# Retiming three edges of a selective scan in a two-layer decoder kernel on one Trainium2 core: a mask step, a bank order and a gate's activations change place

## The reference

```python
# sublayer 1: linear attention, 16 heads of 32
q, k, v = heads(x @ q_w.T + q_b), heads(x @ k_w.T + k_b), heads(x @ v_w.T + v_b)
qp, kp = elu(q) + 1, elu(k) + 1
kv = einsum('bhsd,bhse->bhde', kp, v)
z  = einsum('bhsd,bhd->bhs', qp, kp.sum(axis=2))
x1 = layernorm(x + (einsum('bhsd,bhde->bhse', qp, kv) / (z + 1e-6)) @ o_w.T + o_b)
# sublayer 2: selective scan over the context, gated by silu(x1)
u = silu(causal_conv4(ctx @ in_proj.T) + conv_b)
dt_low, Bm, Cm = split(u @ x_proj.T)              # 16 + 16 + 16 columns
dt = softplus(dt_low @ dt_proj.T + dt_proj_b)
state = state * exp(dt * A) + (dt * u) * B_t      # 512 steps, 512 channels, 16 states
y  = (sum_n state_n * C_n + D * u) * silu(x1)
x2 = layernorm(x1 + y)
```

## Time and profile before

| what | value |
|---|---|
| time, median of 3 runs | 2728.22 us (2726.62 to 2728.88) |
| the profiled execution | 2728.88 us, span 2727.2 us |
| busy share of the span | PE 93%, DVE 71%, ACT 47%, POOL 27% |
| mean granted TensorE clock | 0.974 of full speed |
| the stage of the scans | about 62 to 745 us |
| chain that ended last | PE 53%, DVE 27%, ACT 8%, issue 8%, POOL 3% |

### The profile page before, as it was taken

How to read it: one execution, slowest core, us unless ns; L and a number is a source line. 1 busy time by engine, 2 the same in 40 slices (tenths; PEclk the granted TensorE clock), 3 DMA queues, 4 the chain that set the end, 5 groups by cost and what they waited for, 6 DMA issues and landing times.

```text
span 2727.2 us, 30212 instructions
## 1 busy us (share of the span) xinstructions
PE 2534.4 (93%) x9938; PEld 1675.5 (61%) x9938; DVE 1944.2 (71%) x3609; ACT 1276.6 (47%) x2404; POOL 729.6 (27%) x721
## 2 busy tenths in 40 slices
PE   6999999989779998899999999999999998999997
PEld 2343433434367754577777776777777773688886
DVE  4899999899975578677778787778788785231332
ACT  4464554645433311476746665566646663121111
POOL 1446455556411255221212121121121110000000
PEclk8999999999989999899999999999999999999999
DMA  4112111112320301232323322332332215100000
GB/s 153 54 48 85 51 67 62 56 39 77 116 101 32 124 16 43 108 112 101 139 82 120 109 100 68 100 101 82 102 115 93 78 47 190 51 31 1 31 16 16
DMA packets 81606, 212.51 MB, mean 78 GB/s; under 512 B 8998, under 2 KB 17446, under 8 KB 77356
## 3 DMA queue, kind: packets, MB, share of 16 engines
q1 hardware_dynamic: 73196, 180.88, 20.0%
q0 software_dynamic: 5472, 21.01, 2.0%
q10 hardware_dynamic: 2784, 8.72, 0.9%
HBM read 164.11 MB, written 46.47 MB: 77 GB/s over the span
## 4 chain that ended last, share of the span: by engine, by line
PE 53%; DVE 27%; ACT 8%; issue 8%; POOL 3%; DMA 1%; DVEq 0%; SPq 0%; POOLq 0%; ACTq 0%
PE bank L729 13%; PE bank L1094 10%; DVE h L1890 6%; DVE val L2174 3%; PE bank L1269 3%; PE bank L1270 3%; PE bank L1273 3%; ACT p L1662 3%; DVE val L2167 3%; PE bank L1180 2%; PE bank L944 2%; PE bank L945 2%; PE bank L1203 1%; PE bank L1298 1%; PE bank L1299 1%
## 5 line engine op out<-in xcount | busy, mean ns | idle before, releaser
L2479 POOL TENSOR_TENSOR h<-du,Bb 128x1024 f32<-128x1024 f32 x128 | 313.0, 2448 | 220.8 <-DVE h L1898 220.3
L1890 DVE TENSOR_TENSOR_SCAN h<-bank,h 128x512 f32<-128x512 f32 x256 | 299.7, 1206 | 28.2 <-ACT bank L1443 20.9
L1443 ACT ACTIVATE bank<-dt,A 128x512 f32<-128x512 f32 x256 | 175.1, 690 | 304.2 <-DVE h L1890 302.8
L1662 ACT ACTIVATE p<-bank,sm,rq 128x512 f32<-128x512 f32 x256 | 195.9, 775 | 173.1 <-DVE sm L2303 173.1
L2557 POOL TENSOR_TENSOR rq<-rq,mhalf 128x4 f32<-128x4 f32 x64 | 84.6, 1321 | 690.7 <-DVE rq L2249 690.7
L729 PE MATMUL bank<-pT,v 128*128 128x512 f32 x512 | 230.2, 592 | 0.8 <-ACT pT L1325 0.8
L1898 DVE TENSOR_TENSOR h<-h,Cb 128x1024 f32<-128x1024 f32 x128 | 197.4, 1542 | 6.5
L944 PE MATMUL bank<-h,ident 128*128 128x512 f32 x256 | 148.0, 661 | 53.5 <-DVE h L1898 53.0
L282 POOL TENSOR_SCALAR rstd<-mv 128x1 f32<-128x1 f32 x80 | 23.6, 295 | 647.7 <-DVE mv L276 647.4
L2433 DVE TENSOR_TENSOR h<-bank,sg 128x512 f32<-128x512 f32 (+1 forms) x44 | 30.4, 690 | 227.5 <-PE bank L1273 227.5
L2299 DVE TENSOR_REDUCE sm<-bank 128x1 f32<-128x512 f32 x256 | 164.1, 681 | 2.9 <-PE bank L1094 2.6
(11 more groups left out here) (273 smaller groups left out, 6104.2 us busy)
## 6 DMA issues: line engine op xcount, KB each, us to landing
wxq_s<-wq_dram SPq DMA_DIRECT2D x48, 512.0 KB, 4.0
Bb<-bc_dram SPq DMA_DIRECT2D x32, 512.0 KB, 3.6
Cb<-bc_dram SPq DMA_DIRECT2D x32, 512.0 KB, 3.7
x_dram<-xo POOLq DMA_DIRECT2D x16, 1024.0 KB, 4.8
woh<-in_Wo SPq DMA_DIRECT2D x64, 256.0 KB, 2.6
xc<-x_dram SPq DMA_DIRECT2D x12, 1024.0 KB, 5.5
wxv_s<-wkv_dram SPq DMA_DIRECT2D x12, 1024.0 KB, 5.0
wxk_s<-wkv_dram SPq DMA_DIRECT2D x12, 1024.0 KB, 7.8
```

What stands on the lines that cost most here:

```text
L1443: act.activation(bank[2 + n][:, :], dt[:, c % 2, et, :], ACT.Exp, scale=A[:, et, 2 * w + n:2 * w + n + 1]).then_inc(dA_ready, 1)
L1662: act.activation(p4[:, t, :], bank[4 + t][:, :], ACT.Exp, bias=sm4[:, 4 + t:5 + t], scale=rq[:, hh % 2, 1, t:t + 1], accum_out=sm4[:, 8 + ...
L1890: dve.tensor_tensor_scan(h[:, s, n, :], bank[2 + n][:, :], h[:, s, n, :], 0.0, ALU.mult, ALU.add).then_inc(scanned, 1)
L2479: pool.tensor_tensor(h[:, G % HR, :, :], du[:, et:et + 1, :].to_broadcast([P, 2, S]), Bb[:, w % 2, :, :], ALU.mult).then_inc(dBu_ready, 1)
```

## The change

It has four parts, all in the first stage.

1. DVE masks kv 0 (three pairs of small instructions) after unit 15 and its query step, where it did so between the scans and the C product of unit 15.
2. In the bank order "xdbl" comes behind "kv" 1. PE computes kv 1 in unit 15 and xdbl in unit 16, the reverse of before.
3. On ACT `copy_xdbl` moves from unit 17 to unit 18 and `turned` 2 from unit 19 to unit 18, both behind the exponential n = 1. The four `relu_abs` move one place earlier each: units 20 and 21, after n = 0 and after n = 1.
4. `gate_x1` of a chunk stands at the end of its unit 31, before the exponentials of the next chunk's unit 0, where it stood behind both of them. `value` 2 stands between these two exponentials, where it stood behind both.

```diff
             list0(("q", c, 3), ("kv", c, 0))
             if more:
-                list0(("x", c + 1, 0), ("xdbl", c + 1))
+                list0(("x", c + 1, 0))
             list0(("kv", c, 1))
             if more:
-                list0(("x", c + 1, 1))
+                list0(("xdbl", c + 1), ("x", c + 1, 1))
             list0(("z", c))
...
# PE
-                    if U == 15 and more:
+                    if U == 15:
+                        keys_values(c, 1, (3,))
+                    if U == 16 and more:
                         in_xdbl(c + 1)
-                    if U == 16:
-                        keys_values(c, 1, (3,))
-                        if more:
-                            turn_x(c + 1, 1)
+                        turn_x(c + 1, 1)
...
# ACT, after the exponential n == 0
+                            if U == 0:
+                                value(c, 2)
...
-                            if U in (21, 22) and more:
-                                relu_abs(c + 1, 2 * U - 41)
+                            if U in (20, 21) and more:
+                                relu_abs(c + 1, 2 * U - 40)
...
# ACT, after the exponential n == 1
-                            if U == 0:
-                                if c:
-                                    gate_x1(c - 1)
-                                value(c, 2)
...
-                            if U == 17 and more:
+                            if U == 18 and more:
                                 copy_xdbl(c + 1)
-                            if U == 19 and more:
                                 turned(c + 1, 2)
                             if U in (20, 21) and more:
-                                relu_abs(c + 1, 2 * U - 40)
+                                relu_abs(c + 1, 2 * U - 39)
...
                                 if more:
                                     value(c + 1, 0)
                                     value(c + 1, 1)
-                                else:
-                                    gate_x1(c)
+                                gate_x1(c)
...
# DVE: out of unit(), between the scans and the C product
-                if U == 15:
-                    for g in range(3):
-                        key_value(c, g)
...
# DVE: behind the query step
                     if U == 15:
                         query(c, 3)
+                    if U == 15:
+                        for g in range(3):
+                            key_value(c, g)
```

## The result

| what | before | after |
|---|---|---|
| time, median of 10 runs | 2731.11 us (2726.62 to 2744.24) | 2745.19 us (2736.26 to 2754.51) |
| ratio | | 1.006, 95% interval 1.0042 to 1.0079 |
| profiled execution | 2728.88 us, span 2727.2 | 2739.87 us, span 2738.2 |
| mean granted TensorE clock in it | 0.974 | 0.973 |

The change makes the kernel slower by 0.6%. The ratio counts more executions than the first row: the changed kernel ran 19 times, with a median of 2750.0 us, and the ten of the row by themselves would give 1.005. The forecast was 2734.7 us, in a range that ended at 2743: the sign is right and the size too small.

What follows compares the result with a forecast made beforehand. DVE and PE were both taken as nearly full, with PE's chain binding units 15 to 22. 2 x 1.95 + 0.35 - 0.9 + 3.05 = +6.4 us on 2728.22 gave 2734.7 us, range 2722 to 2743.

Steps and rivals of the forecast that it cites:

- Parts 1 and 2: Units 15 to 19, chunks 0 to 2: z starts 2.25 us later; 1.5 us lost where 1.3 were to be won.
- Anything that makes PE start later there is paid: Units 15 to 22: waits for exponentials are late PE work seen through ACT; PE's kv 1 starts at 145.64.
- Part 4: Three chunk ends: scan 3.7 us late, 2.0 back from a faster C product, 0.51 wait gone; sum +3.05 us.
- Chunk 3: Last chunk: the masks' move hides its wait for kv 0, -0.9 us; bank order and `relu_abs` do not matter.
- the half clock in part 3: Units 20 to 23: one half-clock stretch after z, giving +1.95 us a chunk; without any, +0.7.
- twice the stretch, +3.6: Units 20 to 23: upper end of the cost per chunk, if half clock lasts twice as long.
- rival C: Retimed units: more half clock, PE now standing before z too; +13 us, or +11 with one chunk spared, 2740 us; chance 0.15.
- calmer chunk 2: Chunk 2 was 3.3 us longer than chunk 0; running like it gives -1.3, otherwise +1.95; middle taken, +0.35 us.
- A: Units 15 to 22 and chunk ends: removed waits simply won, at most 19.9 us, 2708 us or some 2718; chance 0.15.
- B: Retimed units: no stretch of half clock there, +1 us in all, 2729 us; chance 0.15.

Runs made afterwards that it cites:

- experiments 5 and 11: Kernel before with kv 0's masks behind unit 15's C product and query step (2743.26 us), or between unit 16's scans and C product (2750.0 us).
- experiment 12: Changed kernel with ACT's copy of xdbl between the two exponentials of unit 18, ahead of the copy of x 1; 2743.13 us, ratio 1.0049.
- experiment 2: Kernel before with only the gate and value 2 moves of part 4; 2734.24 us, ratio 1.0014.
- experiment 1: Changed kernel run and profiled a second time, no edit; 2747.16 us, ratio 1.0056.
- part 2 alone: Kernel before with the new bank order and ACT's copy of xdbl ahead of that of x 1, so z is not held; 2738.87 us, ratio 1.0023.
- without part 4: Changed kernel with the gate and value 2 moves at the chunk ends undone; 2748.62 us, ratio 1.0055.
- experiment 4: Changed kernel with part 1 undone, kv 0's masks again ahead of unit 15's C product; 2745.88 us, ratio 1.0043.
- experiment 8: Changed kernel with nine small matmuls of zeros on PE in unit 15, where it waits for kv 0's bank; 2753.6 us, ratio 1.0051.

## Why the prediction was right in sign and too small

**Parts 1 and 2: the mechanism right, and shown.** "Anything that makes PE start later there is paid": experiments 5 and 11 put it at 1.9 us for 1.88 and 3.4 to 3.7 for 4.11. In the chunks without half clock in front of z, z started 9.09 us after unit 16 did, and the forecast had 154.45 - 145.42 = 9.03. The forecast made the retimed chunk 1.95 us longer at one stretch in both. Measured at equal half clock it is 36.2 - 33.9 = 2.3, and 2.4 counted from unit 15. The missing 0.4 lies behind z: the forecast had PE 2.2 us later there but moved the copy to `zr` by 1.8 only, to 18.33 us after the start of unit 16, and with one stretch it came at 18.89. By parts: 1.7 the masks, 0.4 the bank of z (experiment 12), and some 0.1 for the rest, though part 2 without the hold cost 0.3 by itself. `relu_abs` costs nothing by itself, which the forecast did not separate.

**Part 4: right.** +1.27, +1.26 and +1.1 for 1.03, 1.0 and 1.0, of which about 0.14 is the later start of unit 16 by the masks; alone +1.0 to +1.1 (experiment 2). The page "SBUF — State Buffer" of the Trainium skill (section "🔬 SBUF: two separate sides") held on both sides of the move: 3.26 us beside POOL, 1.23 behind it. The drain of 1.38 us, which the page "ScalarE: Activation LUTs" of the Trainium skill (section "What ACT_TABLE_LOAD costs") adds to each table load, did not appear with the loads on the critical path either: silu started at 235.88, 0.01 us after its load ended.

**Chunk 3: right.** Its kv wait of 0.9 us went; with part 1 alone the way from unit 24 of chunk 2 to unit 16 of chunk 3 took 127.0 us for 127.9.

**The step that failed is the half clock in part 3,** "in all likelihood the clock falls to half for one stretch here", with "twice the stretch, +3.6" as its upper end. In the profiled chunk 0 there were two stretches, one before z, and the chunk cost +4.0, rival C's case. In the second profile chunk 1 has 23.9 us at half clock and costs 9.9 us more than with 3.4; this lay outside both ends. The other side of the same error is chunk 2: I treated its 10.2 us in the one trace as a trait of the chunk, and took -3.3 as possible. The second profile of before had 3.4 there.

**Put together.** By the order alone the change costs 3 x 2.3 - 0.9 + 3.6 = 9.6 us. The terms of the forecast, chunk 2 counted like the others, give 3 x 1.95 - 0.9 + 3.05 = 8.0, so its sizes were 1.6 too small. It then took another 1.6 off for a calmer chunk 2.

The clock comes on top, and here the profiles are few. Windows 16 to 24 of chunks 0 to 2 hold 11.1 us of half clock on average in the four profiles with the order of before there, and 21.6 in the three of the changed kernel: 0.5 x 10.5 = +5.3 us. In chunk 3 it goes the other way, 9.4 us on average before and none after, and its window takes 34.5 and 31.4 us: -3.1. Net this is +2.2 us. The cross attention took 1238.6 and 1241.2 us on average, +2.6, which no edit explains. 9.6 + 2.2 + 2.6 = 14.4.

Measured, the medians differ by 14.1 us in the ten runs of the result (18.9 with all 19) and by 16.0 in experiment 1. Over all executions with a clock on record, 31 of the changed kernel and 70 of the kernel before, the means differ by 15.5 us, and the granted clock gives 161 us at half clock against 156 in the whole kernel: some 5 us more, with an error of 3, so 2 to 3 us of time. That agrees with the net term and not with chunks 0 to 2 alone. So of the 15.5 us about 10 are the order and shown, 2 to 3 are the clock by a rough estimate, and 3 stay open. Of the 9 us by which they exceed the forecast of 6.4, about 4 are the half clock (2 to 3 that came, 1.6 that the forecast took off), 1.6 the sizes, and 3 open.

**Rivals.** A (waits simply won) is out: z started at 156.91, 4.7 us later than in before, 0.7 of it the later start of the stage. B is out: each of the nine windows of chunks 0 to 2 in the three profiles of the changed kernel has a stretch. C named more half clock and came nearest with 2740 us. But the clock's net share was no more than 2 to 3 us, and C stopped at a price per chunk that one window exceeds threefold (47.8 us against 35.6).

**What stays open** is what starts a long stretch. Counted in chunks 0 to 2, windows with 17 us or more at half clock were 0 of 12 in the four profiles with the order of before there, 0 of 3 with part 2 alone, 1 of 3 with part 1 alone, 1 of 9 in the changed kernel, 1 of 3 without part 4, 0 of 3 with xdbl copied first, 2 of 3 without part 1, 2 of 3 with PE filled, 3 of 3 with the masks later still. That speaks for a link with the retimed order, and most with the latest start. In chunk 3, though, the windows with 17 us or more belong to the order of before (1 of 4) and to part 2 alone (1 of 1). Nor is it PE's new idle time alone: experiment 4 does not have it and experiment 8 fills it, and both had two such windows. One thing holds in every case: in the windows of all four chunks, the 13 stretches of 10 us or more begin in unit 20 or 21, where PE works on the matmuls of dt or spread (16 rows by 512 columns). The counts are too small to say more, and whether the changed kernel is really struck more often than the kernel before is not settled.

## What to carry to other kernels

Find the engine whose run bounds the stretch, and ask of every edit whether that engine starts later: here 1.7 us of vector work (a C product and a query step) put in front of it cost 1.9 us a chunk, while three waits of 1.28 us on the vector engine were worth nothing once removed. Where the matrix engine is both the bound and clocked down at times, price an edit from several profiles at equal half clock (time less half of the time at half clock), and keep the clock's part as a range; a single profile gave +11 us where the medians gave +14 and +16. Count the clock over all chunks, too: the three retimed ones alone showed twice the net price.

## What the runs showed of the hardware

- How long the clock stays at 1.2 GHz differs between executions of one program at one place: 3.4, 23.9 and 3.4 us within the window of chunk 1 in three executions of the changed kernel, and a stretch of 17.1 us went on while PE was hardly idle.
- Where PE sets the pace, one us at half clock costs 0.5 us in the scans and 0.43 in the cross attention. Over all unprofiled runs, compared within each kernel, it is 0.42 to 0.44 (from clocks given to three digits).
- The longer PE idled ahead of its run, the more often a stretch at half clock followed within the next units: 0 of 18 windows with 0.33 us, 6 of 18 with 2.21, 3 of 3 with 4.44. Whether filling the 2.2 us with matmuls prevents it is not shown.
- In the windows of the scans the long stretches (10 us and more) all began in unit 20 or 21, 13 of 13, beside matmuls of 16 rows by 512 columns. Two more stretches of 10.2 us began in unit 29 of a chunk 3.
